# A shared-expert split moved from five and six chunks to four and seven, with two DMA streams on other queues

## What is computed

```python
def cond(x, subjects, weights):               # x (64, 64, 512): batch, channel, step
    return jnp.einsum('bct,bcd->bdt', x, weights[subjects])

def ffn(x):                                    # tokens xf: (4096, 512)
    probs = softmax(xf @ gate_w.T)
    top_p, top_i = jax.lax.top_k(probs, 2)
    combine = zeros((n, 8)).at[arange(n)[:, None], top_i].set(top_p)
    h = silu(einsum('nc,efc->enf', xf, expert_fc1)) * einsum('nc,efc->enf', xf, expert_fc2)
    y = einsum('ne,enc->nc', combine, einsum('enf,ecf->enc', h, expert_proj))
    s1, s2 = xf @ shared_fc1.T, xf @ shared_fc2.T          # 1408 wide
    shared = silu(s1) * s2 @ shared_proj.T
    return y + sigmoid(xf @ shared_gate_w.T) * shared

out = x + ffn(cond(x))
```

## Time and profile before

| | us |
|---|---|
| median of 3 runs | 1246.27 (1244.6 to 1247.4) |
| profiled execution | 1248.22 |
| its span, first to last instruction | 1246.3 |
| TensorE busy | 1233.0 (99%) |
| VectorE, ScalarE, GpSimd busy | 821.5, 461.8, 264.9 |

### The profile page before, as it was taken

The page is one execution under the profiler, slowest core; times in us unless marked ns, Lnnn a source line. Parts: engine busy times, 40 slices in busy tenths (PEclk is TensorE's granted clock), DMA queues, the critical chain, the costliest instruction groups (busy, mean ns, idle before and its releaser), DMA issues.

```text
span 1246.3 us, 17284 instructions
## 1 busy us (share of the span) xinstructions
PE 1233.0 (99%) x6206; PEld 1027.1 (82%) x6206; DVE 821.5 (66%) x1331; ACT 461.8 (37%) x765; POOL 264.9 (21%) x356
## 2 busy tenths in 40 slices
PE   9999999999999999999999999999989999999998
PEld 6888888888888899988888888889868887887887
DVE  6445554469754877776666665557677778788675
ACT  5223231221011566665555555446304214213211
POOL 4277773000001111111111111110240130130110
PEclk9999999999999999999999999999999999999999
DMA  9487876202215677686666666644894885885842
GB/s 342 154 291 283 313 279 251 91 37 102 101 37 211 228 246 259 227 280 209 212 206 208 214 214 200 236 138 149 288 339 128 310 259 164 284 262 157 307 128 96
DMA packets 105411, 262.94 MB, mean 211 GB/s; under 512 B 11090, under 2 KB 11218, under 8 KB 100850
## 3 DMA queue, kind: packets, MB, share of 16 engines
q1 hardware_dynamic: 67602, 164.74, 37.2%
q0 software_dynamic: 13872, 54.27, 13.0%
q10 hardware_dynamic: 23856, 42.87, 10.9%
HBM read 195.52 MB, written 66.32 MB: 210 GB/s over the span
## 4 chain that ended last, share of the span: by engine, by line
PE 92%; DVE 4%; DMA 2%; issue 1%; ACT 1%; SPq 0%; DVEq 0%; ACTq 0%
PE bank_h L938 42%; PE bank_o L938 23%; PE bank_h L1197 10%; PE bank_t L1197 8%; PE bank_t L915 2%; PE bank_h L1079 2%; DMA picked<-xf_transposed 2%; PE bank_t L938 2%; PE bank_t L862 1%; PE bank_o L872 1%; PE bank_h L872 0%; DMA picked<-x 0%; PE bank_h L854 0%; PE bank_t L1043 0%; PE bank_h L1149 0%
## 5 line engine op out<-in xcount | busy, mean ns | idle before, releaser
L938 PE MATMUL bank_h<-x_hi,w_hi 128*128 128x512 f32 (+1 forms) x768 | 278.7, 363 | 0.2
L938 PE MATMUL bank_h<-x_hi,w_lo 128*128 128x512 f32 (+1 forms) x768 | 272.2, 354 | 0.0
L938 PE MATMUL bank_h<-x_lo,w_hi 128*128 128x512 f32 (+1 forms) x768 | 272.1, 354 | 0.0
L820 POOL DMA_INDIRECT rows<-xf_rows,token_of x71 | 69.2, 974 | 550.4 <-PE bank_t L915 372.8
L938 PE MATMUL bank_o<-wp_hi,h_hi 128*128 128x512 f32 (+1 forms) x442 | 180.7, 409 | 0.2 <-DVE h_lo L1727 0.2
L938 PE MATMUL bank_o<-wp_lo,h_hi 128*128 128x512 f32 (+1 forms) x442 | 177.9, 403 | 0.0
L938 PE MATMUL bank_o<-wp_hi,h_lo 128*128 128x512 f32 (+1 forms) x442 | 177.2, 401 | 0.0
L938 PEld LDWEIGHTS bank_h<-x_hi,w_lo 128*128 128x128 f32 x768 | 145.2, 189 | 20.6
L938 PEld LDWEIGHTS bank_h<-x_hi,w_hi 128*128 128x128 f32 x768 | 145.5, 189 | 19.2 <-DVE x_lo L1731 0.9
L938 PEld LDWEIGHTS bank_h<-x_lo,w_hi 128*128 128x128 f32 x768 | 145.5, 189 | 17.6
L1304 ACT ACTIVATE g_sb<-bank_h 128x512 f32<-128x512 f32 x40 | 23.9, 598 | 249.4 <-PE bank_h L938 249.4
(11 more groups left out here) (269 smaller groups left out, 2327.5 us busy)
## 6 DMA issues: line engine op xcount, KB each, us to landing
raw<-ew SPq DMA_DIRECT2D x29, 1408.0 KB, 6.7
w_early<-late_up ACTq DMA_DIRECT2D x69, 256.0 KB
slot_rows<-res SPq DMA_DIRECT2D x32, 512.0 KB, 3.3
rawp<-ewp SPq DMA_DIRECT2D x29, 512.0 KB, 7.1
x_hi<-late_up ACTq DMA_DIRECT2D x46, 256.0 KB, 3.9
x_lo<-late_up ACTq DMA_DIRECT2D x46, 256.0 KB
xt_in<-xf_transposed SPq DMA_DIRECT2D x11, 1024.0 KB, 7.5
late_up<-raw POOLq DMA_DIRECT2D x6, 1792.0 KB, 8.5
```

The lines of the kernel that those rows point to most:

```text
L820: pool.indirect_dma_start(rows[:, row % 4, :], None, xf_dram, bass.IndirectOffsetOnAxis(token_of[:, HALF_OF[row]:HALF_OF[row] + 1].bitcast ...
L938: mm = pe.matmul(dst, a, m, start=(first and i == 0), stop=(last and i == 2))
```

## The change

- `PARTS` becomes 4 early and 7 late chunks. The late chunks of a group are now a team of three, a middle chunk whose eight down rows are made alone inside the two chunks after it, and another team of three. The middle chunk's down weights share a slot with those of chunk 0 and are loaded again for every group.
- The front's matmuls are placed at fixed steps of a block (`MAPS_AT`: the map of slot k comes after steps 4, 9, 14, 19, 25, 31, 39 and 47 of 48), transposes and router matmuls two at a time. The down rows 0 and 1 go together.
- The store of `rows` is issued by ScalarE after its own copy, no longer by SyncE.
- In blocks 0 to 2 the result rows are stored and the next block's rows loaded by GpSimd: `result_rows` ahead of slot 4 of the next block, `next_result_rows` ahead of its slot 7.
- GpSimd prepares one late chunk in four slots instead of three, from `PREP` = 8 on, and the seventh after its loop. The split of the sums is done in two halves.
- VectorE's token sums and picks move into the late chunks, between two of the combining additions. The late input load stands ahead of the load of the late down weights. Routing steps are spread anew over blocks 4 to 7, which have four chunks each.

```diff
-PARTS = [list(range(0, 5)), list(range(5, 11))]
+PARTS = [list(range(0, 4)), list(range(4, 11))]
+MAPS_AT = ((4, 9, 14, 19, 25, 31, 39, 47), (7, 12, 17, 21, 26, 31, 39, 47))
+STEPS = 2 * KC * len(PARTS[0])
-PREP = TILES - 3 * LATE
+PREP = TILES - 4 * (LATE - 1)
...
@@ SyncE
                     front_load(t + 4, k % 4)
-                front_store(t, k % 4)
...
                 if slots < SLOTS:
                     front_store_xt(TILES - 1, 1)
-                store_res(0, b)
-                sp.wait_ge(res_stored, 16 * (b + 1))
-                load_res(0, b + 1)
+                    store_res(0, b)
+                    sp.wait_ge(res_stored, 16)
+                    load_res(0, b + 1)
...
-                    if j == TEAM - 1 and b == 0:
-                        load_late_wp(1)
                     if j == TEAM - 1 and b + 1 < HBLOCKS:
                         sp.wait_ge(late.x_lo, PRODUCTS * (b + 1))
                         for t in range(2):
                             load_late_x(b + 1, t)
+                    if j == MIDDLE and b == 0:
+                        load_late_wp(2, MIDDLE + 1, TEAM)
...
@@ GpSimd
+            def result_rows(b):
+                pool.wait_ge(shared[0].o_kept, BT * (b + 1))
+                nc.gpsimd.dma_start(part_dram[b * BN:(b + 1) * BN, :]..., res[:, :, :]).then_inc(front_res_out, 16)
+            def next_result_rows(b):
+                pool.wait_ge(front_res_out, 16 * b)
+                nc.gpsimd.dma_start(res[:, :, :], x_rows[b * BN:(b + 1) * BN, :]...).then_inc(front_res_in, 16)
             for t in range(LEAD, TILES):
-                j, part = divmod(t - PREP - 1, 3)
+                b, k = divmod(t - LEAD, SLOTS)
+                if b and k == 4:
+                    result_rows(b - 1)
+                if b and k == 7:
+                    next_result_rows(b)
+                j, part = divmod(t - PREP - 1, 4)
...
                 elif t >= PREP and part == 1:
                     late_split_sums(j)
+                elif t >= PREP and part == 2:
                     late_split_raw(j)
                 elif t >= PREP:
                     late_split_down(j)
+            result_rows(FULL - 1)
+            late_sums(LATE - 1)
+            next_result_rows(FULL)
+            late_split_sums(LATE - 1)
+            late_split_raw(LATE - 1)
+            late_split_down(LATE - 1)
...
@@ TensorE
+                order = [(r, j) for r in range(2) for j in range(chunks - 1)] + [(r, chunks - 1) for r in range(2)] + [
+                    (r, j) for r in range(2, BT) for j in range(chunks)]
+                for step, (r, j) in enumerate(order):
+                    if j == 0:
+                        at_least(pe, f.o_kept, b * BT + r - 1)
...
+                late_chunk(b * LATE + MIDDLE)
+                late_chunk(b * LATE + MIDDLE + 1, ((), (), (0,), (1,), (2,), (3,), (4,)))
+                late_chunk(b * LATE + MIDDLE + 2, ((5,), (6,), (7,), (), (), (), ()))
+                late_chunk(b * LATE + MIDDLE + 3)
...
@@ ScalarE
                 copy(rows[:, k % 4, :], bank[:, :]).then_inc(frow_ready, 1)
+                if not (isinstance(stores, int) and stores == 0):
+                    act.wait_ge(frow_ready, t + 1)
+                    nc.scalar.dma_start(xf_dram[bass.ds(t * P, P), :], rows[:, k % 4, :]).then_inc(frow_stored[k % 4], 16)
...
@@ VectorE, slot 6 of a front block
+                    if k == 6:
+                        dve.wait_ge(gate_ready, b + 1)
+                        if first:
+                            dve.wait_ge(res_loaded, 16)
+                        else:
+                            dve.wait_ge(front_res_in, 16 * b)
+                        for r in range(2):
+                            row_sum(0, b, r)
...
                 nc.vector.tensor_tensor(h2_sb, bank_h[1][:, :], u3_sb, ALU.add).then_inc(late.c22, 1)
+                if between:
+                    between()
```

More of the change, by code:

```diff
@@ L890, in _, with front_lead_routes, front_step @@
                     front_map(t + 2, t + 2, bank_h[t + 2])
-            def front_piece(b, k, c, bank, slots):
-                t = LEAD + SLOTS * b + k
[L895 to L899, removed]
+            def front_lead_routes(k):
+                for c in range(KC):
+                    front_route(LEAD + k - 2, k, c, bank_o[1], xt_in[:, LEAD + k - 2, c * P:(c + 1) * P])
+            def front_step(b, step, slots):
+                first = isinstance(b, int) and b == 0
+                maps = MAPS_AT[first]
+                k = next(q for q in range(SLOTS) if step <= maps[q])
+                begin, end = maps[k - 1] + 1 if k else 0, maps[k]
+                t = LEAD + SLOTS * b + k
+                at = step - begin
+                if k <= slots and at in (1, 2):
+                    for c in (2 * at - 2, 2 * at - 1):
+                        front_transpose(t - 1, k - 1, c, bank_t[1])
+                if k <= slots + 1 and step >= end - 1:
+                    if step == STEPS + 6:
+                        pe.wait_ge(shared[0].h_mul, len(PARTS[0]) * (b + 1))
+                    bank = bank_h[3] if step > STEPS or k == 0 else bank_o[1]
+                    for c in (2 * (step - end) + 2, 2 * (step - end) + 3):
+                        front_route(t - 2, k - 2, c, bank, xt_in[:, t - 2, c * P:(c + 1) * P] if first and k < 2 else None)
+                if k < slots and step == end:
+                    front_slot_map(b, k)
             def front_slot_map(b, k):
@@ L1314, in block_gate, with shared_step @@
                 nc.scalar.activation(s_gate[:, ts], logits[:, E, ts], ACT.Sigmoid).then_inc(gate_ready, 1)
-            def shared_step(n, b, ahead=0, front=0, gate=True):
-                gates(n, b, ahead, front)
+            def shared_step(n, b, front=0, gate=True):
+                gates(n, b, front)
                 if n == 0 and gate:
                     block_gate(b)
-                late = SLOTS - 1 if front == SLOTS else len(PARTS[0])
-                for k in range(len(PARTS[0]), late):
+                late = 7 if isinstance(b, int) and b == 0 else 6
+                for k in range(5, min(late, front)):
                     front_slot(b, k)
@@ L1756, in hiddens, with front_block @@
+            def hiddens(n, b, between=None):
+                for j in range(len(PARTS[n])):
+                    one_hidden(n, b, j)
                     if between:
                         between(j)
+            def front_block(b, slots):
+                first = isinstance(b, int) and b == 0
+                for k in range(SLOTS):
+                    if k == 6:
+                        one_hidden(0, b, 3)
+                    slot_fx(b, k, slots)
+                    if first and k in (0, 3):
+                        split_shared(0, 3 if k else 2)
+                    if first and k in (1, 4):
+                        one_hidden(0, b, k // 2)
+                    slot_xt(b, k, slots)
+                    if first and k == 7:
+                        rest_xt(0, 1)
+                    if first and k == 2:
+                        one_hidden(0, b, 1)
+                    elif not first and k in (1, 3, 4):
+                        one_hidden(0, b, k // 2 if k < 4 else 2)
+                    if k == 6:
+                        dve.wait_ge(gate_ready, b + 1)
[5 more added lines that the diff above has]
+                            row_sum(0, b, r)
+                    if k == 7:
+                        row_sum(0, b, 2)
+                    slot_logits(b, k, slots)
+                    if k == 6 and not first:
+                        rest_xt(0, b + 1)
+                row_sum(0, b, 3)
```

319 lines of the change are left out of this document (178 added, 141 removed).

## The result

The changed kernel took a median of 1264.14 us (1262.91 to 1264.98, 4 runs), the kernel before 1246.05 on the same chip: 1.0146 times as long, 95% interval 1.0121 to 1.0172. Forecast were 1249 and a range of 1235 to 1257. The direction was right and the size was not: the span grew by 16.9 us (1246.3 to 1263.2) where the sum had +3.1. Beside the experiments the runs of the kernel before lay between 1241.78 and 1250.1 us, so its profiled execution of 1248.22 is one of the longer ones, and the medians differ by more (18.1 us here, 20.4 in `e9_after_again`) than the two spans.

The account below looks back on a forecast made before the run. TensorE, busy 1233.0 of 1246.3 us, was taken as the bound. Matmuls -5.4, late stage -10.0 and front +18.5 gave +3.1, put on the runs' median of 1246.27: 1249.4, forecast 1249 us, range 1235 to 1257.

Parts of the forecast that it names:

- the sum: Whole span of 1246.3 us: matmuls -5.4, late stage -10.0, front +18.5, together +3.1 us.
- the mechanism, the place, the landing: Block 1, row 2: TensorE 15.9 us late for result rows on GpSimd's queue, landing some 11.5 us after issue.
- Matmuls -5.4: Moving a chunk from early to late: 288 matmuls become 264, taking 5.4 us off TensorE.
- ScalarE's store: Front slots: its added wait and issue (0.54 to 0.57 us) fit the slot, except at the sigmoid's table load.
- the routing blocks: Blocks 4 to 7: routing loses 33 us of cover; costed at 0, with 3 as upper end.
- The 0.6 for the sigmoid: Blocks 0 to 2: table load ahead of slot 5's copy costs 0.6 us each; only block 2's stays.
- the price of GpSimd's chunk, 24.65 us: Front: a late chunk in four slots takes GpSimd 24.65 us, as TensorE's four slots; slot 7 of block 1 at 109.2.
- block 2: no second wait: Block 2: GpSimd issues the result-row load 50 us later, as long as TensorE's block, so no wait.
- the third rival: Front: GpSimd's chunk takes 2 us more; slot 7 of block 1 5 later, block 2 waits 4 more: 1258; chance 0.22.
- the late stage, 10.0 of 10.9 gained: Four late groups: earlier token load and sums between additions regain 10.0 of the 10.9 us lost.
- the slow clock behind the long wait: Block 1, after TensorE's long wait for result rows: the lower clock costs 2 us.
- The second rival: Front: GpSimd keeps its lead, 11 us gained before slot 7 of block 1: 1234; chance 0.28.

Follow-up runs that it names:

- e9_after_again: The changed kernel as it is, measured again beside the kernel before on one chip: 1264.87 us, ratio 1.0164.
- e6_load_first: `e2_early_start` with the result-row load issued just ahead of the 1.8 MB `late_up` store instead of behind it and the raw load: 1245.35 us, ratio 1.0000.
- e7_sync_stores: `e3_both` with the front rows' stores moved back from ScalarE's queue to SyncE's: 1237.59 us, ratio 0.9942.
- e3_both: Changed kernel with result rows stored and loaded two slots earlier on GpSimd's queue, plus the earlier preparation start of `e2_early_start`: 1236.94 us, ratio 0.9940.
- e4_before_swap: Kernel before, with the next group's token tiles loaded ahead of the second set of down weights in SyncE's late loop: 1242.27 us, ratio 0.9981.
- e2_early_start: Changed kernel with GpSimd's late preparation started earlier, its first raw load waiting for three weight pieces, not all eight: 1255.36 us, ratio 1.0085.
- e8_sync_rows_early_start: Changed kernel with front result rows back on SyncE's queue, plus the earlier preparation start of `e2_early_start`: 1239.22 us, ratio 0.9957.

## Why the prediction was right and wrong

**Right: the mechanism, the place, the landing.** TensorE waits over 8 us at row 2 of block 1 for a `row_sum` that a DMA from `x` into `res` on GpSimd's queue releases; the clock is at its lower level behind it. The landing was 11.8 against 11.5 (the terms as they stand, 8.9 - 0.5 + 3.6 for 1 MB, make 12.0), and `e6_load_first` shows the reason given for it, the queue, in numbers: 12.3 and 13.2 behind the store, 7.8 and 7.2 ahead of it. By the Trainium skill, DMA: Bandwidth & Descriptors, section "Two DMAs through the same engine are not ordered", descriptors within one queue of one DMA engine start in order; these runs agree. Matmuls -5.4, ScalarE's store (nothing in `e7_sync_stores`) and the routing blocks (no loss) held as well. The 0.6 for the sigmoid in each block was too much: the waits for the copy are 0.2 to 0.3 each.

**Failed step 1: the price of GpSimd's chunk, 24.65 us.** Slot 7 of block 1 came at 113.99 instead of 109.2, and TensorE went on at 126.6 instead of 121.6: 5.0 us. Of the 4.8, 1.7 are the start: the split of the early weights ended at 37.6 (37.4 said), but the raw load, taken at its best of 5.0, was issued at 38.26 and the sums began at 44.46, so they and their issues ended at 48.9 and not 47.2:

```profile
44.46 0.73 POOL L765 TENSOR_TENSOR raw<-raw 128x256 f32<-128x256 f32 x1 [3.53 <-DMA raw<-sw]
```

The other 3.1 are the chunk. Between the starts of the sums at 44.46, 69.68, 95.78, 122.05, 148.87 and 176.74 lie 25.2, 26.1, 26.3, 26.8 and 27.9 us. The term that was mis-sized is the slot's casts. They were taken from one occurrence, 118.59 to 120.07, as 1.48, and that is one of the shortest. Timeline of GpSimd before: the gap inside an earlier set, then the two gaps of the set that was taken:

```profile
107.85 0.23 POOL L798 CAST wp_hi<-h_hi 64x64 fp32r x1 [0.97 <-issue]
...
118.81 0.23 POOL L798 CAST wp_hi<-h_hi 64x64 fp32r x1 [0.22 <-issue]
...
119.59 0.23 POOL L798 CAST wp_hi<-h_hi 64x64 fp32r x1 [0.38 <-issue]
```

From the end of the instruction before to the end of the last cast the mean over the 13 full sets between 95 and 202 us of the trace of before that did not wait for TensorE is 2.24 (1.42 to 3.70), and over 17 of after 2.27. The idle was in the earlier trace rows, 15.8 us over 24 gaps, and I used it for a rival only. With 2.24 a chunk with its result DMA is 22.47 + 2.24 + 0.7 + 0.57 = 26.0, near the 26.1 and 26.3 of the two chunks of block 1, and the way to slot 7, with four such slots in it (one for each chunk and two behind), gets 4 x 0.76 = 3.0 longer. On the way itself the two sets behind the chunks took 3.03 and 2.00, which is 2.1 of the 3.1.

**Failed step 2: "block 2: no second wait".** It rested on GpSimd's two chunks being as long as TensorE's block. From 113.99 to 168.25 they took 54.3, TensorE needed 52.8 from 126.6 to row 2 at 179.4, its slow clock included, and the landing was 2 us longer. Timeline of TensorE:

```profile
179.04 0.40 PE L997 MATMUL bank_t<-w_hi,wp_lo 128*128 128x512 f32 x1
182.87 0.50 PE L997 MATMUL bank_o<-wp_hi,h_hi 128*128 128x512 f32 x1 [3.43 <-DVE res L1884]
```

From the map of slot 6 to that of slot 7 it took 12.8 us where `e3_both`, without the wait, took 7.6: 5.2 lost, 3.4 of them the wait and 1.8 the slow clock behind it. These are the effects of the third rival, "slot 7 of block 1 comes 5 later and block 2 waits 4 more", almost to the us; it had 0.22. Its reason, denser engines beside GpSimd, is not what made slot 7 of block 1 late: the casts took the same in both kernels (2.24 and 2.27). In the way from there to block 2 it may have a part: 54.3 is 2.3 more than two chunks of 26.0, and one subtract that met VectorE's (last section) makes 1.9 of that.

**Failed step 3: the late stage, 10.0 of 10.9 gained.** 6.5 were. The long wait went, and the first group lost 2.0 instead of 8.8. But the later two lost 1.2 each where they had lost 1.1 and 1.0, so moving their sums gained nothing; a wait of 0.8 to 0.9 for an addition is left in each. And 1.3 of the first group's 2.0 are new: at its end TensorE waits twice for a `row_sum`, 0.3 and 1.0 us, each behind a pick of 1.5 us; the change put two picks there where one was. Timelines of VectorE and TensorE:

```profile
935.44 1.53 DVE L2073 SCALAR_TENSOR_TENSOR rawp<-h_sb,p_top,rawp 128x512 f32<-128x512 f32 x2
```
```profile
938.94 0.50 PE L997 MATMUL bank_o<-wp_hi,h_hi 128*128 128x512 f32 x1 [1.03 <-DVE res L2138]
```

Of the long wait `e4_before_swap` shows that the load's place alone is worth 4.2 of 6.2 us and that VectorE's order held the rest. That this rest went by the sum's move behind the addition is argued from the code, not tested.

5.0 + 5.2 + 3.5 are 13.7 of the 13.8 by which the span missed the sum (16.9 against 3.1). That they meet so closely is partly luck: the slow clock behind the long wait cost some 2.8 and not 2, the sigmoid's 0.6 is not there, and the plain blocks were 0.7 quicker.

**Missed and of no account for the sum:** TensorE stood 2.4 us in block 0 for the map of slot 5, with 2.5 of slow clock (10.4 us from this map to the next, 7.9 in `e3_both`). Timelines of TensorE and GpSimd:

```profile
50.88 0.77 PE L997 MATMUL bank_t<-w_hi,wp_hi 128*128 128x512 f32 x1 [2.40 <-issue]
```
```profile
50.05 0.73 POOL L834 CAST wp_lo<-h_lo 64x64 fp32r x1
```

The profile calls the releaser "issue", but the cast ended 0.1 us ahead: GpSimd's start had eaten the whole lead by then. In the changed kernel this vanishes in the long wait, as the text said of such waits; once the place is mended it is what is left, with the three waits of 1.6 in all, and the earlier start saves both (1242.2 to 1236.9).

**The second rival** (GpSimd keeps its lead, 1234) was wrong for this kernel. It asked for 11 us gained on GpSimd, slot 7 near 98 instead of 109.2. No run reached that with the old order: in `e2_early_start` the load came at 104.71 and a wait of 7 us was left.

## What to carry to other kernels

A DMA that another engine waits for inherits the whole program of the engine that issues it: ask what stands ahead of it in that order, in time and in bytes, and place it by when its data are needed, not by the slot that was free. When two engines take turns over a ring, price a step from the end of the step before, averaged over many, since on an engine with no slack the gaps are the price. And a long wait can have two limits, one behind the other: in `e4_before_swap` the transfer was mended, and the order of VectorE's program still held the same matmul for 2.0 us.

## What the runs showed of the hardware

**GpSimd and VectorE block each other.** When VectorE went on after the long wait, the same GpSimd subtract that takes 1.25 to 1.8 us elsewhere in that trace took 3.19. Timeline of after, VectorE, then GpSimd:

```profile
127.19 2.50 DVE L1831 TENSOR_TENSOR x_lo<-xt_in,x_hi 128x2048 fp32r<-128x2048 f32 x1
129.61 1.76 DVE L1632 TENSOR_TENSOR w_lo<-picked,w_hi 128x512 fp32r<-128x512 f32 x1
```
```profile
127.62 3.19 POOL L777 TENSOR_TENSOR raw<-raw 128x512 fp32r<-128x512 f32 x1
```

GpSimd's ends 1.1 us after VectorE's first, and VectorE's second, mostly 0.69 us (at most 1.39) elsewhere, takes 1.76 and ends about 0.6 us after GpSimd's. The Trainium skill, SBUF — State Buffer, section "SBUF: two separate sides", has the two engines share one port pair as an exclusive lock for a whole instruction, where VectorE's has two inputs in SBUF and GpSimd's reads SBUF, as here; the rows agree. It lengthens GpSimd's chunk just where it is late already. This one subtract took 1.9 us longer than the 1.3 of most of them; how much such meetings cost over the whole front was not measured.

**The clock after a wait.** The length of the wait alone did not tell in these runs whether the clock falls. Windows behind a wait of 1.4 us in `e8_sync_rows_early_start` and behind one of 2.0 us in `e4_before_swap`:

```profile
66.50:70.50 4.00, 4.00 (x12) 3.01 (x13) 1.86 (x4) 0.24 (x1) 3.75 (x6) 0.57 0.91 289
```
```profile
928.30:932.00 3.70, 3.70 (x17) 3.05 (x18) 3.13 (x5) 1.26 (x2) 0.00 (x0) 1.00 0.85 300
```

The first ran near the 1.2 GHz level, the second at full clock. In `e6_load_first` the clock was 1.00 in the 4 us behind a wait of 1.7 us and 0.64 behind one of 1.8. A wait of 1.4 to 3.4 us was so followed by a loss of up to 2.5 us more, or by none; what decides was not tested.
